# Attention and routing block on one core: values of four head pairs projected in 512-column float32r matmuls, z scaled in mid-oct, last scatters two pairs later

## The chip, the cores and the metric

The kernel runs on one core of a Trainium2 chip. The number that counts is the device time of one execution in microseconds (us). All engines of the core work in parallel and are ordered by hand with semaphores: PE (TensorE, matrix products), DVE (VectorE), ACT (ScalarE), POOL (GpSimd) and SP (SyncE, which issues most DMAs).

## The reference

```python
# x (4, 1024, 128), w_q, w_k, w_v (16 heads, 128, 64), w_o (1024, 128)
q, k, v = (einsum('bsd,hdk->bhsk', x, w) for w in (w_q, w_k, w_v))
weights = softmax(einsum('bhqk,bhmk->bhqm', q, k) / sqrt(64), axis=-1)
z = einsum('bhqm,bhmk->bhqk', weights, v)      # heads side by side: (b, s, 1024)
attn = x + einsum('bse,ed->bsd', z, w_o)
# router: softmax(xf @ Wr), argmax over 8 experts, rank of a token within its expert,
# 512 slots an expert, two matmuls with relu per expert, scaled by the share, added back
x = x + attn(layernorm(x));  x = x + ffn(layernorm(x))
```

All of it is in float32. Where the kernel has a product in the type float32r (F32R) it first splits both factors in a high part and the rest, and adds three products: high by rest, rest by high and high by high.

## The kernel before

The 4 batches have 16 heads each. A **pair** is two heads of a batch, so there are 32 pairs, numbered 0 to 31, eight to a batch. `in_order` runs the function `pair(j, par, b)` of every engine for j from 0 to 31; `par` is j modulo 2 and names the buffers.

A pair has four **octs**: octs 0 and 1 belong to the first 512 queries of both heads, octs 2 and 3 to the last 512, and an oct takes half of the 1024 keys. In an oct PE makes eight `scores` (128 keys by 512 queries of one head, two matmuls of 512 columns, lines 1335 and 1336), ACT takes their exponentials into `ring` (line 784), POOL adds them up over the keys (`add_up`, line 628, fourteen adds a pair), and PE multiplies them by V (`values`, line 1349). Between these stands work for later pairs. In order, an oct of PE is:

- scores 0 to 2; `project_qk`, queries and keys of pair j+2 (lines 1259 to 1261, three F32R matmuls of 512 columns); scores 3 and 4
- in octs 0 and 2 `project_v`: half of V of pair j+1 (line 1268, four plain float32 matmuls of 128 columns); in octs 1 and 3 `project_out` (line 1382) of an earlier pair
- scores 5 to 7; `visit`, four matmuls of `max_scores` (line 1283) for the row maxima of pair j+1; the sixteen matmuls of `values`; a second `visit`. In oct 0 also `softmax_sums` (line 1367).

The two visits of an oct and `project_qk`, `project_v` and `project_out` lend each other the same PSUM banks (`ps_m`: `lent_max`, `lent_out`, `lent_turn`). A visit may start when DVE's `reduce_max` (line 1023) has read what the visit before it left, and `project_qk` waits for all reductions so far (`maxed`).

DVE in an oct: two reductions for each visit (line 1023), `low_qk` (line 1014, the rest of queries or keys, after ACT's `cast_qk`, line 737), in octs 1 and 3 `add_out` (line 1043). It also takes the reciprocals of the softmax sums in four quarters a pair (`recip`, line 1028) and multiplies z by them (`scale_z(j, h)`, line 1037, h being the half of the queries). Between the two, SP spreads the reciprocals over partitions (`spread_sums`, line 473, eight DMAs). Before the change `scale_z(j - 1, 0)` stands behind the second reductions of oct 3, and `scale_z(j - 2, 1)` behind those of oct 0.

SP loads, in each pair, the weights of pair j+2 (`load_weights`, lines 395 to 397: w_q, w_k and w_v, 64 KB each), and then issues the `place` DMAs (lines 448 to 455), which carry the queries and keys from `qk_high` and `qk_rest` to the four operand buffers; six follow a cast. SP takes its work in order, and so a DMA issued before them delays them. The buffers `qk_high` are two, so the next cast (line 737) waits until the DMAs that read the last but one have ended; the last of these is line 451, keysB.

Tokens are normalised for a batch before its pairs (`early(j, ahead)` says for which). After a batch's pairs its second half, the router, follows within later pairs. `routed(j, role)` gives the batch whose step `role` falls into pair j: moments are `a`, roots `b`, turning and logits `c` (DVE then: `choose`, lines 970 to 976, and `shift`, line 1093), ranks and four scatters `d` (`find_slots`, lines 991 to 996), four more scatters `e`, all three batches two pairs apart. `ROUTE_FROM` is the pair of the first `a`.

```python
        def early(j, ahead):
            return j + ahead if 1 <= j + ahead < B else None
        ROUTE_FROM = PAIRS - 9
```

At the start, before pair 0, PE makes the first row maxima and runs idle matmuls (`spin`, line 1241) while transfers are under way.

## Time and profile before

| what | value |
| --- | --- |
| three runs | 1523.64, 1524.18, 1525.06 us (median 1524.18) |
| the profiled execution's time | 1522.48 us |
| its span (first to last instruction) | 1520.5 us |
| mean granted TensorE clock | 0.993 |
| busy: PE, POOL, DVE, ACT | 1488.0, 1209.4, 976.2, 793.2 us |

The span is the stretch that the profile shows; the execution's own time has 2.0 us more around it. Rows are given as start us, duration us, engine, line, operation, tile written <- tiles read, and in square brackets the idle time of the engine ahead of the row and what released it. PE's matmuls overlap, so a row of PE is read by its start: the next row's start less its own is what it costs.

### The profile page before, as it was taken

To read this page: it belongs to the slowest core of one execution; us is meant where nothing else is said; L and a number is where in the kernel's file an instruction comes from. 1 tells how busy PE (TensorE), PEld (TensorE's weight loads), DVE (VectorE), ACT (ScalarE), POOL (GpSimd) and SP (SyncE) were. 2 spreads that over 40 slices of the span, in tenths; PEclk is the share of its full clock that TensorE was granted. 3 is DMA by queue.
4 is the path that set the end of the run, shared out by engine and by line. 5 is a ranking of instruction groups with operands and counts; after the bars stand their busy time and mean duration, and the time that the engine had idled before them with its cause. 6 is when DMAs were issued, how large, how long until landed. Compare 5 with 4: busy or idle time off the path is not lost.

```text
span 1520.5 us, 22014 instructions
## 1 busy us (share of the span) xinstructions
PE 1488.0 (98%) x7472; PEld 863.8 (57%) x7472; DVE 976.2 (64%) x1236; ACT 793.2 (52%) x1549; POOL 1209.4 (80%) x672
## 2 busy tenths in 40 slices
PE   8999999999999999999999999999999999999896
PEld 5555555555555555555555555555555555555485
DVE  6667665666666666676666656667667676666552
ACT  4566645455555555555546454555554555545341
POOL 5889877798777777798777777888877989979544
PEclk9999999999999999999999999999999999999898
DMA  6334444443344443432344444433443443340420
GB/s 146 87 77 94 109 99 103 107 100 71 80 97 101 108 92 84 98 84 66 89 102 99 102 94 91 91 77 72 97 101 86 112 95 82 74 97 15 137 79 32
DMA packets 125518, 137.90 MB, mean 91 GB/s; under 512 B 44330, under 2 KB 69421, under 8 KB 125408
## 3 DMA queue, kind: packets, MB, share of 16 engines
q1 hardware_dynamic: 119008, 130.26, 37.2%
q0 software_dynamic: 2048, 4.10, 0.8%
q10 hardware_dynamic: 4352, 2.13, 0.5%
q8 instruction: 61, 1.00, 0.3%
q14 instruction: 49, 0.40, 0.1%
HBM read 16.81 MB, written 8.45 MB: 17 GB/s over the span
## 4 chain that ended last, share of the span: by engine, by line
PE 92%; DVE 3%; POOL 2%; issue 1%; ACT 1%; another core or an unknown queue 0%; DMA 0%; POOLq 0%; ACTq 0%; DVEq 0%
PE ps_w L1349 28%; PE ps_w L1335 17%; PE ps_w L1336 15%; PE ps_m L1283 11%; PE ps_m L1268 4%; PE ps_m L1382 4%; PE ps_w L1367 2%; PE ps_m L1259 2%; PE ps_m L1260 2%; PE ps_m L1261 2%; DVE mxw L1023 1%; POOL acc L628 1%; DVE z L1037 1%; PE ps_w L1622 1%; PE ps_w L1683 1%
## 5 line engine op out<-in xcount | busy, mean ns | idle before, releaser
L628 POOL TENSOR_TENSOR acc<-acc,ring 128x1024 f32<-128x1024 f32 x382 | 917.6, 2402 | 51.3 <-ACT ring L784 3.4
L1023 DVE TENSOR_REDUCE mxw<-ps_m 128x1 f32<-128x1024 f32 x512 | 602.9, 1219 | 356.4 <-PE ps_m L1283 352.0
L784 ACT ACTIVATE ring<-ps_w 128x512 f32<-128x512 f32 x1024 | 544.7, 597 | 246.4 <-PE ps_w L1336 244.2
L1349 PE MATMUL ps_w<-ring,V 128*64 128x512 f32 x2048 | 467.7, 598 | 0.0
L1335 PE MATMUL ps_w<-queriesA,keysA 128*128 128x512 f32 x1024 | 432.3, 422 | 2.0 <-ACT ring L784 1.1
L1336 PE MATMUL ps_w<-queriesB,keysB 65*128 65x512 f32 x1024 | 406.9, 397 | 0.0
L628 POOL TENSOR_TENSOR acc<-ring 128x1024 f32<-128x1024 f32 x64 | 152.2, 2378 | 180.1 <-PE ps_w L1367 172.3
L1349 PEld LDWEIGHTS ps_w<-ring,V 128*64 128x64 f32 x2048 | 135.8, 136 | 265.4 <-issue 228.2
L1335 PEld LDWEIGHTS ps_w<-queriesA,keysA 128*128 128x128 f32 x1024 | 194.4, 190 | 90.1 <-issue 49.4
L1336 PEld LDWEIGHTS ps_w<-queriesB,keysB 65*128 65x128 f32 x1024 | 194.9, 190 | 34.1 <-issue 0.7
L1283 PE MATMUL ps_m<-keysA,queriesA 64*128 64x512 f32 x1000 | 182.9, 443 | 0.8 <-DVE one_hot_b L976 0.6
L1283 PEld LDWEIGHTS ps_m<-keysA,queriesA 64*128 64x128 f32 x1000 | 74.5, 184 | 149.0 <-issue 147.6
L764 ACT ACTIVATE z<-ps_w 128x512 f32<-128x512 f32 x64 | 38.2, 597 | 221.6 <-PE ps_w L1349 221.6
L1014 DVE TENSOR_TENSOR qk_rest<-ps_m,qk_high 128x512 fp32r<-128x512 f32 x123 | 85.1, 692 | 92.7 <-ACT qk_high L737 83.0
L1028 DVE RECIPROCAL sums<-sums 128x128 f32<-128x128 f32 x128 | 116.4, 931 | 0.0
L775 ACT ACTIVATE sums<-ps_w 128x512 f32<-128x512 f32 x33 | 19.7, 597 | 129.7 <-PE ps_w L1367 115.4
L737 ACT ACTIVATE qk_high<-ps_m 128x512 fp32r<-128x512 f32 x123 | 73.5, 598 | 10.7 <-PE ps_m L1261 3.3
L1382 PEld LDWEIGHTS ps_m<-wo,z 128*128 128x128 f32 x496 | 65.0, 191 | 6.4 <-DVE mxw L1023 1.0
L1268 PEld LDWEIGHTS ps_m<-wst,hT 128*128 128x128 f32 x496 | 65.1, 191 | 5.7 <-DVE mxw L1023 0.2
L1382 PE MATMUL ps_m<-wo,z 128*128 128x128 f32 x496 | 65.6, 275 | 0.1
L1268 PE MATMUL ps_m<-wst,hT 128*128 128x128 f32 x496 | 65.5, 275 | 0.0
L664 POOL DMA_INDIRECT out<-ye,ring x32 | 31.1, 972 | 33.2 <-DVE ye L1192 26.4
(193 smaller groups left out, 974.6 us busy)
## 6 DMA issues: line engine op xcount, KB each, us to landing
queriesA<-qk_high SPq DMA_DIRECT2D x248, 128.0 KB
keysB<-qk_high SPq DMA_DIRECT2D x124, 128.0 KB
keysA<-qk_rest SPq DMA_DIRECT2D x124, 128.0 KB
queriesB<-qk_rest SPq DMA_DIRECT2D x124, 128.0 KB
by_sums<-sums SPq DMA_DIRECT2D x240, 64.0 KB, 2.0
keysA<-qk_high SPq DMA_DIRECT2D x93, 128.0 KB
tokens_by_slot<-blank ACTq DMA_DIRECT2D x16, 130.0 KB, 3.2
ring<-tokens_by_slot SPq DMA_DIRECT2D x8, 260.0 KB, 5.5
```

Source lines behind the costliest of these rows:

```text
L628: pool.tensor_tensor(acc[h][:, :], before, P_both(kt), ALU.add).then_inc(summed, 1)
L737: act.activation(qk_high[s][:, :], bank, ACT.Copy).then_inc(qk_cast, 1)
L784: act.activation(P_tile(kt, p), ps_s[k % 3][:, :], ACT.Exp, scale=SCALE).then_inc(exp_done, 1)
L1014: dve.tensor_tensor(qk_rest[s][:, :], qk_bank(j, use), qk_high[s][:, :].bitcast(F32), ALU.subtract).then_inc(qk_low, 1)
L1023: dve.tensor_reduce(mxw[h][:, p * HT + qt:p * HT + qt + 1], ps_m[p][:, :], AX_X, ALU.max).then_inc(maxed, 1)
L1028: dve.reciprocal(sums[:, c], sums[:, c]).then_inc(recip_done, 1)
L1268: mm = pe.matmul(bank[:, i * P:(i + 1) * P], hT[:, t:t + P], wst[par][:, 4 * DK:6 * DK], start=True, stop=True)
L1283: mm = pe.matmul(ps_m[p][:, kh * HALF:(kh + 1) * HALF], queriesA[par][p][r, at:at + P], keysA[par][p][r, kh * HALF:(kh + 1) * HALF], start ...
L1335: pe.matmul(ps_s[k % 3][:, :], keysA[par][p][:, t], queriesA[par][p][:, c], start=True, stop=False)
L1336: pe.matmul(ps_s[k % 3][:, :], keysB[par][p][:, t], queriesB[par][p][:, c], start=False, stop=True).then_inc(scores_ready, 1)
L1349: mm = pe.matmul(ps_z[p * DK:(p + 1) * DK, :], V[par][:, kt * P + p * DK:kt * P + (p + 1) * DK], P_tile(kt, p), start=(kt == 0), stop=(kt ...
L1382: mm = pe.matmul(bank[:, i * P:(i + 1) * P], z[j % 2][h][:, i * P:(i + 1) * P], wo[j % 3][:, :], start=True, stop=True)
```

## The change

- From pair 4 on V is not made pair by pair. For each group of four pairs `project_tile(g, t, bank)` makes V of a tile of 128 tokens for all four pairs at once: three F32R matmuls with 512 columns, for eight tiles a group. Six tiles stand in the last pair of the group before (two in octs 0 and 2, one in octs 1 and 3), two in oct 0 of the group's first pair. A tile in `lent_max` stands between scores 3 and 4, one in `lent_out` or `lent_turn` behind scores 4. The other octs have nothing in that place but `project_out`. Pairs 0 to 3 are as before.
- w_v of a group is loaded by `load_group` (64 and 192 KB) in the pairs 1, 5, ..., 25, between `load_weights` and the `place` DMAs; `load_weights` itself has one DMA less and waits for `w_low_split`. ACT splits a group's w_v in oct 1 of the pairs 2, 6, ..., 26 (`split_high_values`), POOL at h=1, kt=2 of the same pairs (`split_low_values`). `V` is one buffer with five places.
- `scale_z(j - 2, 0)` stands in mid oct 0 and `scale_z(j - 2, 1)` in mid oct 2, behind `low_qk` and ahead of the second reductions. `recip` of the last quarter moves from oct 1 to mid oct 2.
- `h_rows` is one buffer and hT holds two batches; the normalisation of batches 1, 2 and 3 falls into pairs 4b-4 to 4b-2, with four pairs between batches.
- `ROUTE_FROM` is 22 and no longer 23: `a` to `d` come one pair earlier, `e` stays where it was, two pairs behind `d`.
- Ahead of pair 0 the spins are 5 and 1 and no longer 9 and 3.

```diff
-        h_rows = [sb(f"h_rows{i}", [P, QT, D]) for i in range(2)]
+        h_rows = sb("h_rows", [P, QT, D])
...
-        hT = sb("hT", [P, T])
+        hT = sb("hT", [P, 2 * S])
...
-        V = [sb(f"V{i}", [P, KT * P]) for i in range(2)]
+        V = sb("V", [P, 5 * KT * P])
+        wv = sb("wv", [P, 4 * P])
+        wv_high, wv_low = (sb(n, [P, 4 * P], F32R) for n in ("wv_high", "wv_low"))
...
         def early(j, ahead):
-            return j + ahead if 1 <= j + ahead < B else None
...
-        ROUTE_FROM = PAIRS - 9
+            b, odd = divmod(j + ahead + 3, GROUP)
+            return b if odd == 0 and 1 <= b < B else None
+        GROUP = 4
+        GROUPS = PAIRS // GROUP
+        IN_LAST = {0: [(0, lent_max), (1, lent_out)], 1: [(2, lent_turn)], 2: [(3, lent_max), (4, lent_out)],
+                   3: [(5, lent_turn)]}
+        IN_FIRST = {0: [(6, lent_max), (7, lent_out)]}
+        def single_values(j):
+            return j < GROUP
+        def value_tiles(j, oct):
+            g, i = divmod(j, GROUP)
+            if i == GROUP - 1 and g + 1 < GROUPS:
+                return [(g + 1, t, bank) for t, bank in IN_LAST[oct]]
+            return [(g, t, bank) for t, bank in IN_FIRST.get(oct, [])] if i == 0 and g > 0 else []
+        def values_no(g, t):
+            return KT * g + t + 1
+        def place_of(j):
+            g, i = divmod(j, GROUP)
+            return 0 if g % 2 == 1 and i == GROUP - 1 else 1 + i
+        def V_of(j, kt, p):
+            at = (place_of(j) * KT + kt) * P + p * DK
+            return V[:, at:at + DK]
+        def loads_of(j):
+            k = j // 2
+            return 48 * min(k + 1, GROUP // 2) + 32 * max(k + 1 - GROUP // 2, 0)
+        ROUTE_FROM = PAIRS - 10
         def routed(j, role):
-            b, odd = divmod(j - ROUTE_FROM - "abcde".index(role), 2)
+            b, odd = divmod(j - ROUTE_FROM - "abcd-e".index(role), 2)
             return b if odd == 0 and 0 <= b < B - 1 else None
...
                     view = wst[par][:, 0:4 * DK].rearrange("p (t h k) -> p h t k", h=2, t=2)
                 sp.dma_start(view[:, :, 0, :], wq_d[:, 2 * hp:2 * hp + 2, :]).then_inc(w_loaded[par], 16)
                 sp.dma_start(view[:, :, 1, :], wk_d[:, 2 * hp:2 * hp + 2, :]).then_inc(w_loaded[par], 16)
-                sp.dma_start(wst[par][:, 4 * DK:6 * DK].rearrange("p (h k) -> p h k", h=2),
-                             wv_d[:, 2 * hp:2 * hp + 2, :]).then_inc(w_loaded[par], 16)
+                if single_values(j):
+                    sp.dma_start(wst[par][:, 4 * DK:6 * DK].rearrange("p (h k) -> p h k", h=2),
+                                 wv_d[:, 2 * hp:2 * hp + 2, :]).then_inc(w_loaded[par], 16)
+            def load_group(g):
+                h = 2 * GROUP * (g % 2)
+                order = [(h, 2), (h + 2, 6)] if g % 2 == 0 else [(h + 6, 2), (h, 6)]
+                if g > 1:
+                    sp.wait_ge(wv_low_split, g - 1)
+                for c, (h, n) in zip((slice(0, P), slice(P, 4 * P)), order):
+                    sp.dma_start(wv[:, c].rearrange("p (h k) -> p h k", h=n),
+                                 wv_d[:, h:h + n, :]).then_inc(wv_loaded, 16)
...
-                    sp.wait_ge(v_done, 2 * j + 2)
+                    if single_values(j):
+                        sp.wait_ge(v_done, 2 * j + 2)
+                    else:
+                        sp.wait_ge(w_low_split, j - 1)
                     load_weights(j + 2, par)
+                if j % GROUP == 1 and (j + 3) // GROUP < GROUPS:
+                    load_group((j + 3) // GROUP)
...
             def split_low_tokens(b, g):
                 pool.wait_ge(high_split, 2 * b + g + 1)
-                c, at = slice(g * HALF, (g + 1) * HALF), b * S + g * HALF
-                pool.tensor_tensor(h_low[:, c], hT[:, at:at + HALF], h_high[:, c].bitcast(F32),
+                c = slice(g * HALF, (g + 1) * HALF)
+                pool.tensor_tensor(h_low[:, c], hT_of(b, g), h_high[:, c].bitcast(F32),
...
+            def split_low_values(g):
+                pool.wait_ge(wv_high_split, g)
+                pool.tensor_tensor(wv_low[:, :], wv[:, :], wv_high[:, :].bitcast(F32),
+                                   ALU.subtract).then_inc(wv_low_split, 1)
...
                         if routed(j, "d") is not None and h == 1 and kt % 2 == 1:
                             scatter(routed(j, "d"), [kt // 2])
+                        if j % GROUP == 2 and (j + 2) // GROUP < GROUPS and (h, kt) == (1, 2):
+                            split_low_values((j + 2) // GROUP)
                         if routed(j, "e") is not None and (h, kt) == (0, 1):
...
+                    act.wait_ge(low_split, 2 * (b - 1))
+                    act.wait_ge(v_done, 2 * GROUP)
+                act.activation(hT_of(b, g), turn_bank(b, g), ACT.Copy).then_inc(hT_ready, 1)
...
+                act.wait_ge(residual_ready, b)
+                act.wait_ge(h_turned, 2 * b)
...
@@ -745,13 +815,28 @@
                 act.wait_ge(hT_ready, 2 * b + g + 1)
                 if b > 0:
                     act.wait_ge(qk_done, 4 * HP * b - 2 + 2 * g)
-                c, at = slice(g * HALF, (g + 1) * HALF), b * S + g * HALF
-                act.activation(h_high[:, c], hT[:, at:at + HALF], ACT.Copy).then_inc(high_split, 1)
+                    act.wait_ge(v_done, values_no(2 * b - 1, KT - 1))
+                c = slice(g * HALF, (g + 1) * HALF)
+                act.activation(h_high[:, c], hT_of(b, g), ACT.Copy).then_inc(high_split, 1)
...
             def copy_v(j, par, half, bank):
                 act.wait_ge(v_done, 2 * j + half + 1)
-                act.activation(V[par][:, half * HALF:(half + 1) * HALF], bank,
-                               ACT.Copy).then_inc(v_copied, 1)
+                at = place_of(j) * KT * P + half * HALF
+                act.activation(V[:, at:at + HALF], bank, ACT.Copy).then_inc(v_copied, 1)
...
+            def split_high_values(g):
+                act.wait_ge(wv_loaded, 32 * g)
+                if g > 1:
+                    act.wait_ge(v_done, values_no(g - 1, KT - 1))
+                act.activation(wv_high[:, :], wv[:, :], ACT.Copy).then_inc(wv_high_split, 1)
+            def copy_v_tile(g, t, bank):
+                act.wait_ge(pv_done, OCTS * (GROUP * g - 1))
+                act.wait_ge(v_done, values_no(g, t))
+                at = 1 - g % 2
+                act.activation(V[:, :].rearrange("p (s k c) -> p s k c", s=5, k=KT)[:, at:at + GROUP, t, :],
+                               bank.rearrange("p (s c) -> p s c", s=GROUP), ACT.Copy).then_inc(v_copied, 1)
...
-                    if oct in (0, 2) and not last:
+                    if oct in (0, 2) and single_values(j + 1):
                         copy_v(j + 1, nxt, oct // 2, lent_out)
+                    for made in value_tiles(j, oct):
+                        copy_v_tile(*made)
...
+                    if j % GROUP == 2 and (j + 2) // GROUP < GROUPS and oct == 1:
+                        split_high_values((j + 2) // GROUP)
...
+                    if oct in (0, 2) and j >= 2 and not last:
+                        scale_z(j - 2, oct // 2)
+                    if oct == 2 and not first and not last:
+                        recip(j - 1, 1, 3)
...
-                    if oct == 0 and j >= 2:
+                    if oct == 0 and last:
                         scale_z(j - 2, 1)
-                    if oct == (0 if last else 3) and not first:
+                        scale_z(j - 1, 0)
+                    if oct == 3 and known(j, LAST - 1):
                         scale_z(j - 1, 0)
                     if oct == 1 and not first:
                         recip(j - 1, 1, 2)
+                    if oct == 1 and last:
                         recip(j - 1, 1, 3)
...
+            def project_tile(g, t, bank):
+                b, c = GROUP * g // HP, slice(t * P, (t + 1) * P)
+                pe.wait_ge(wv_low_split, g)
+                pe.wait_ge(low_split, 2 * b + t // HT + 1)
+                pe.matmul(bank, h_low[:, c], wv_high[:, :], start=True, stop=False)
+                pe.matmul(bank, h_high[:, c], wv_low[:, :], start=False, stop=False)
+                pe.matmul(bank, h_high[:, c], wv_high[:, :], start=False, stop=True).then_inc(v_done, 1)
...
-                if oct == 0:
+                if single_values(j) and oct == 0:
                     pe.wait_ge(v_copied, 2 * j + 2)
+                elif not single_values(j) and oct < 2:
+                    pe.wait_ge(v_copied, values_no(j // GROUP, (HT if oct == 0 else KT) - 1))
...
                         mm = pe.matmul(ps_z[p * DK:(p + 1) * DK, :],
-                                       V[par][:, kt * P + p * DK:kt * P + (p + 1) * DK], P_tile(kt, p),
+                                       V_of(j, kt, p), P_tile(kt, p),
...
-                    if not last and oct in (0, 2):
+                    if oct in (0, 2) and single_values(j + 1):
                         project_v(j + 1, nxt, oct // 2, next_b, lent_out)
+                    for made in tiles:
+                        if made[2] is not lent_max:
+                            project_tile(*made)
...
-                        if not last and oct in (0, 2):
+                        if oct in (0, 2) and single_values(j + 1):
                             pe.wait_ge(v_copied, 2 * (j + 1) + oct // 2 + 1)
+                        for g, t, _ in tiles:
+                            pe.wait_ge(v_copied, values_no(g, t))
...
-            spin(9, ps_s[0])
+            spin(5, ps_s[0])
             first_visit(5, 1)
-            spin(3, ps_s[0])
+            spin(1, ps_s[0])```

PE in oct 0 of pair 3, behind the last matmul of `project_qk`; L1335 and L1336 (L1439 and L1440) are scores, L1268 is `project_v`, L1372 to L1374 are `project_tile`. Before:

```order
L1261 MATMUL ps_m<-h_high,w_high 128x512
L1335 MATMUL ps_w<-queriesA,keysA 128x512
L1336 MATMUL ps_w<-queriesB,keysB 128x512
L1335 MATMUL ps_w<-queriesA,keysA 128x512
L1336 MATMUL ps_w<-queriesB,keysB 128x512
L1268 MATMUL ps_m<-wst,hT 128x128 x4
L1335 MATMUL ps_w<-queriesA,keysA 128x512
```

Now:

```order
L1357 MATMUL ps_m<-h_high,w_high 128x512
L1439 MATMUL ps_w<-queriesA,keysA 128x512
L1440 MATMUL ps_w<-queriesB,keysB 128x512
L1372 MATMUL ps_m<-wv_high,h_low 128x512
L1373 MATMUL ps_m<-wv_low,h_high 128x512
L1374 MATMUL ps_m<-wv_high,h_high 128x512
L1439 MATMUL ps_w<-queriesA,keysA 128x512
L1440 MATMUL ps_w<-queriesB,keysB 128x512
L1372 MATMUL ps_m<-wv_high,h_low 128x512
L1373 MATMUL ps_m<-wv_low,h_high 128x512
L1374 MATMUL ps_m<-wv_high,h_high 128x512
L1439 MATMUL ps_w<-queriesA,keysA 128x512
```

The four short matmuls behind scores 4 are gone, and two tiles of three long ones stand ahead of and behind scores 4.

DVE from the end of oct 1 to the second reductions of oct 2 in an early pair; L1028 (L1117) is `recip`, L1023 (L1112) `reduce_max`, L1014 (L1103) `low_qk`, L1126 `scale_z`. Before:

```order
L1028 RECIPROCAL sums<-sums 128x128 [waits sums_copied] x2
L1023 TENSOR_REDUCE mxw<-ps_m 128x1 [waits m_done1]
L1023 TENSOR_REDUCE mxw<-ps_m 128x1 [waits m_done0]
L1014 TENSOR_TENSOR qk_rest<-ps_m,qk_high 128x512 [waits qk_cast,low_placed0]
L1023 TENSOR_REDUCE mxw<-ps_m 128x1 [waits m_done1]
```

Now:

```order
L1117 RECIPROCAL sums<-sums 128x128 [waits sums_copied]
L1112 TENSOR_REDUCE mxw<-ps_m 128x1 [waits m_done1]
L1112 TENSOR_REDUCE mxw<-ps_m 128x1 [waits m_done0]
L1103 TENSOR_TENSOR qk_rest<-ps_m,qk_high 128x512 [waits qk_cast,low_placed0]
L1126 TENSOR_TENSOR z<-by_sums,z 128x512 [waits z_copied,spread1]
L1117 RECIPROCAL sums<-sums 128x128 [waits sums_copied]
L1112 TENSOR_REDUCE mxw<-ps_m 128x1 [waits m_done1]
```

One reciprocal has gone from the end of oct 1 to mid oct 2, and a `scale_z` stands there ahead of it.

SP in pair 5, from `place_max` (L461, L518) to the first `place` DMAs (L448 and L449, L505 and L506). Before:

```order
L461 DMA queriesB<-mxt 1x4x128
L395 DMA wst<-in_L_attn_w_q 128x2x64 [waits v_done]
L396 DMA wst<-in_L_attn_w_k 128x2x64
L397 DMA wst<-in_L_attn_w_v 128x2x64
L448 DMA keysA<-qk_high 64x512 [waits qk_cast,scores_ready]
```

Now:

```order
L518 DMA queriesB<-mxt 1x4x128
L440 DMA wst<-in_L_attn_w_q 128x2x64 [waits w_low_split]
L441 DMA wst<-in_L_attn_w_k 128x2x64
L453 DMA wv<-in_L_attn_w_v 128x2x64 [waits wv_low_split]
L453 DMA wv<-in_L_attn_w_v 128x6x64
L505 DMA keysA<-qk_high 64x512 [waits qk_cast,scores_ready]
```

The pair's own w_v load has gone, and two loads of a group's w_v stand ahead of the `place` DMAs.

## Rows read from the trace of the kernel before

**Rows 1.** The page, busy time of the engines over the span

```profile
PE 1488.0 (98%) x7472; PEld 863.8 (57%) x7472; DVE 976.2 (64%) x1236; ACT 793.2 (52%) x1549; POOL 1209.4 (80%) x672
```

**Rows 2.** Busy by window: steady pair 13, and an oct without projections

```profile
603.22:646.23 43.01, 43.01 (x216) 24.42 (x216) 27.60 (x28) 23.59 (x47) 34.17 (x16) 1.00 0.39 87
62.98:72.69 9.71, 9.71 (x46) 4.96 (x44) 5.50 (x7) 4.70 (x10) 9.07 (x5) 1.00 0.17 39
```

**Rows 3.** Timeline of PE, oct 2 of pair 13

```profile
615.72 0.39 PE L1259 MATMUL ps_m<-h_high,w_low 128*128 128x512 f32 x1
...
616.42 0.40 PE L1335 MATMUL ps_w<-queriesA,keysA 128*128 128x512 f32 x1
...
617.35 1.05 PE L1268 MATMUL ps_m<-wst,hT 128*128 128x128 f32 x8
...
618.48 0.40 PE L1336 MATMUL ps_w<-queriesB,keysB 65*128 65x512 f32 x1
...
619.74 0.73 PE L1283 MATMUL ps_m<-keysA,queriesA 64*128 64x512 f32 x4
...
623.98 0.73 PE L1283 MATMUL ps_m<-keysA,queriesA 64*128 64x512 f32 x4
```

**Rows 4.** Timeline of DVE in the same pair

```profile
612.39 1.75 DVE L1028 RECIPROCAL sums<-sums 128x128 f32<-128x128 f32 x2
...
617.40 0.69 DVE L1014 TENSOR_TENSOR qk_rest<-ps_m,qk_high 128x512 fp32r<-128x512 f32 x1 [0.74 <-ACT qk_high L737]
...
643.78 0.68 DVE L1037 TENSOR_TENSOR z<-by_sums,z 128x512 f32<-128x512 f32 x1
```

**Rows 5.** Timeline of POOL in the same pair

```profile
611.31 9.93 POOL L628 TENSOR_TENSOR acc<-acc,ring 128x1024 f32<-128x1024 f32 x4
...
646.23 2.39 POOL L628 TENSOR_TENSOR acc<-ring 128x1024 f32<-128x1024 f32 x1 [7.26 <-PE ps_w L1367]
```

**Rows 6.** Timeline of DVE and POOL in pair 14, where tokens are split

```profile
675.17 1.26 POOL L616 TENSOR_TENSOR h_low<-hT,h_high 128x512 fp32r<-128x512 f32 x1
676.39 2.93 DVE L1037 TENSOR_TENSOR z<-by_sums,z 128x512 f32<-128x512 f32 x1
676.40 7.68 POOL L628 TENSOR_TENSOR acc<-acc,ring 128x1024 f32<-128x1024 f32 x3
```

**Rows 7.** Timeline, SP's queue and ACT, start of pair 14

```profile
631.87 0.60 SPq L397 DMA_DIRECT2D wst<-in_L_attn_w_v  x1
...
634.44 0.60 SPq L451 DMA_DIRECT2D keysB<-qk_high  x1
...
637.70 0.60 ACT L737 ACTIVATE qk_high<-ps_m 128x512 fp32r<-128x512 f32 x1
```

**Rows 8.** The same at the start of pair 27

```profile
1198.71 0.60 SPq L451 DMA_DIRECT2D keysB<-qk_high  x1
...
1201.57 0.60 ACT L737 ACTIVATE qk_high<-ps_m 128x512 fp32r<-128x512 f32 x1 [0.68 <-DMA keysB<-qk_high]
```

**Rows 9.** Timeline of DVE and PE at `choose` of the first batch

```profile
1137.87 0.22 DVE L970 TENSOR_REDUCE routing_columns<-ps_m 128x8 f32<-128x64 f32 x1 [2.04 <-PE ps_m L1403]
...
1139.53 0.73 PE L1283 MATMUL ps_m<-keysA,queriesA 64*128 64x512 f32 x4 [0.20 <-DVE one_hot_b L976]
```

**Rows 10.** Timeline of DVE and PE at `find_slots` of the first batch

```profile
1160.42 0.17 DVE L996 SCALAR_TENSOR_TENSOR scatter_at<-ps_m,routing_columns 128x8 int32<-128x8 f32 x1
...
1161.00 0.73 PE L1283 MATMUL ps_m<-keysA,queriesA 64*128 64x512 f32 x4
```

**Rows 11.** Timeline of POOL in pair 28, and the last four scatters of a batch

```profile
1256.45 2.39 POOL L628 TENSOR_TENSOR acc<-ring 128x1024 f32<-128x1024 f32 x1 [4.32 <-PE ps_w L1367]
...
1296.81 0.99 POOL L603 DMA_INDIRECT tokens_by_slot<-x,scatter_at  x1 [0.17 <-issue]
...
1301.63 2.41 POOL L628 TENSOR_TENSOR acc<-ring 128x1024 f32<-128x1024 f32 x1
```

**Rows 12.** Timeline at the start, PE's spins and SP's queue

```profile
25.79 2.17 PE L1241 MATMUL ps_w<-ident 128*128 128x128 f32 x18
26.28 1.36 SPq L461 DMA_DIRECT2D queriesB<-mxt  x2
27.68 0.53 SPq L448 DMA_DIRECT2D keysA<-qk_high  x1
```

**Rows 13.** Waits of PE: waiter, releaser, total us, times, longest

```profile
PE ps_m L1259 <- DVE mxw L1023: 1.6, 4, 0.6
```

26 lines of the change are left out of this document (17 added, 9 removed).

## The prediction

> **What bounds the kernel now.** I read the page's busy times first, then a window of one steady pair, then the timelines of the engines in it, then the waits. PE is busy for 1488.0 of 1520.5 us [rows 1]. In the steady pair it is busy for all of its 43.01 us, at full clock, while DVE is busy for 27.60, ACT for 23.59 and POOL for 34.17 [rows 2]. So what PE issues sets the pace, and time taken from PE's stream is time gained for as long as no other engine is late. The timelines show how near the others are. POOL stands idle for 7.26 us before each pair's first add [rows 5]. ACT makes the cast of line 737 in its turn [rows 7], and only in one of the shown places does it wait 0.68 for a transfer [rows 8]. DVE has its slack around the visits, and PE waits for it in few places [rows 9, 13].
>
> The sum below is made against the profiled execution, 1522.5 us. The median of the runs shown, 1524.2, is 1.7 above it, and I add that at the end.
>
> **1. Project_v against project_tile (PE, the gain).** In the steady pair project_v starts at 617.35 and the score behind it, whose first matmul overlaps it, has its second one at 618.48. Three plain score steps of 0.23 in their row (615.72 to 616.42 is three matmuls, 0.70 us) put the price of project_v at 1.13 less 0.23, about 0.89 [rows 3]. As a check: an oct without it takes 9.71 [rows 2] and the mean oct of the pair, which holds half a project_v, half a project_out and a project_qk, 10.75. A tile of three F32R matmuls of 512 columns has the very shape of project_qk, 0.70 [rows 3]. 56 halves go (28 pairs with two) and 56 tiles come (7 groups of 8), so the gain is 56 x (0.885 - 0.70) = **-10.4**. Bounds: -8.4 (0.85 for the one) to -11.2 (0.90).
>
> That row also bears on a rule of the Trainium skill ("TensorE: Matmul & The Clock Gate", Back-to-back issue gap), which gives about 81 ns for a sustained matmul of 128 columns and 131 ns for one of 512. By it the same swap would gain 56 x (8 x 0.081 - 3 x 0.131) = 14.3 us, an estimate. The trace has 234 ns for 512 columns of this float32r kind and does not agree, so the rule enters nothing.
>
> **2. Spins at the start.** 18 records take 2.17 us [rows 12], two to a spin, so 6 fewer spins are 12 records, 1.45 us. But the first scores also need the transfers of place_max, issued from 26.28 and followed by the place DMAs [rows 12]. The bounds are -1.45 and 0; I take the middle, **-0.7**.
>
> **3. Waits for z.** PE waits 1.6 us in four places ahead of project_qk for the last reduction [rows 13], some of them behind a slow scale_z at an oct's end. With z scaled in mid-oct these can go: **-1.0**, between 0 and -1.6.
>
> **4. The group's loads.** In the pairs 1, 5, ..., 25 SP issues two DMAs where it issued one, 0.64 us an issue (four of them lie between 631.87 and 634.44) [rows 7]. Everything behind them on SP is late by that: the six place DMAs. The last of them that a cast waits for is keysB. In the steady case it is issued at 634.44 and the cast runs at 637.70, 3.26 later [rows 7]. In the late case issue to cast is 2.86, with a wait of 0.68 [rows 8]. So the slack is 0.4, and 0.64 - 0.4 = 0.25 us of lateness is left. A late cast holds back ACT's next exponentials, and PE's score 6 waits for them, one to one. Seven loads: 7 x 0.25 = **+1.8**. Below: 0, if ACT's own backlog hides it. Above: the 192 KB are ahead of keysB in the queues; if they add a full us, 1.3 for each, 9 in all.
>
> **5. Scale_z in mid oct 2.** This is the change's dangerous place. Scale_z takes 0.68 when POOL is idle, but 2.93 at 676.39, where an add of POOL began at 676.40 [rows 4, 6]. It is done about 0.6 after the add that was running has ended, so it waits for POOL's running instruction. In oct 2 POOL always adds. The steady pair: low_qk ends at 617.40 + 0.69 = 618.09; POOL's four adds from 611.31 take 2.48 each [rows 5], so a boundary is at 611.31 + 3 x 2.48 = 618.76, 0.67 later. Scale_z would be done at 618.76 + 0.68 = 619.44, and the reciprocal (1.75 / 2 = 0.88) [rows 4] at 620.32. With project_v gone, both visits come 0.89 earlier, the next at 623.98 - 0.89 = 623.09 [rows 3]. Two reductions of 2.36 in all, from 620.32, end at 622.7. That leaves 0.4 us: **0** in the steady pair. The work that hides it is PE's sixteen values matmuls. If scale_z comes over 0.67 later, it misses that boundary, loses 2.48 more, and the visit waits 2.48 - 0.4 = 2.1.
>
> A rule of the Trainium skill ("GPSIMD Engine Reference", § 8 Key points) says that GpSimd shares its SBUF interfaces with VectorE, and that this tells on VectorE instructions with two SBUF inputs. The trace agrees: scale_z is one, 2.93 against 0.68 us. It speaks against this change, and the prices here and in the rivals are taken from the rows alone.
>
> Where the phase is not the steady one:
> - Pairs 6, 14 and 22 split tokens: line 616 takes 1.26 of POOL in mid-oct [rows 6] and moves the boundary by as much. I put the end of the reductions 0.7 behind the visit, 3 x 0.7 = **+2.1** (0 to 2.4 in all, then other boundaries are met).
> - Pairs 24, 26 and 28 have `choose` and `shift` in oct 2. Before, DVE was idle for 2.04 ahead of choose, and PE's visit still waited for 0.20 [rows 9]. The logits now come 0.89 earlier, but scale_z with its wait and the reciprocal, 0.67 + 0.68 + 0.88 = 2.2, come first. 2.2 + 0.2 - 2.04 + a part of 0.89 makes between 0.4 and 1.2: 0.7 x 3 = **+2.1**; a missed boundary in all three would make it 8.
> - Pairs 25, 27 and 29 have find_slots in oct 0, with slack 161.00 - 160.59 = 0.4 (both + 1000) [rows 10]. Where there is no tile (25 and 29) the visit comes 0.89 earlier and scale_z adds 0.68 less what DVE idled: 0.7 x 2 = **+1.4**; 0 to 2.3.
>
> **6. POOL.** POOL keeps its work, so with the pair shorter by at most 1.8 its idle time falls from 7.26 to about 5.5, and by a few tenths more for the adds that scale_z touches. Both groups of four scatters now fall into the pairs 27 and 29: 45.2 us from 1256.45 to 1301.63 for adds and eight scatters, against 43.0 - 1.8 = 41.2 for pair 29. The excess of 4.0 meets the 4.32 of idle before it [rows 11]: **+0.3**, at most 4.
>
> **7. What costs nothing.** The tiles' copies on ACT (0.60) replace those of V. The splits of w_v on ACT and POOL (once a group, about 1 us) lie in POOL's idle time and ACT's 19 us a pair. A tile in lent_max ahead of scores 4 waits for reductions that end 0.2 before it by the steady timeline; it is bounded by 0 and 0.3 a tile, for 14 tiles 4 us, and I take 0. Hidden by ACT's three queued exponentials.
>
> **Sum.** -10.4 - 0.7 - 1.0 + 1.8 + 2.1 + 2.1 + 1.4 + 0.3 = -4.4. 1522.5 - 4.4 = 1518.1 for a profiled execution, 1518.1 + 1.7 = **1519.8** for the median.
>
> **Rivals.**
> - *All stalls are hidden.* DVE and ACT queue up differently once PE is faster, and a stall in one oct gives the next more slack. Then 4, 5 and 6 fall to 0 or 1: -12.1, so 1512 to 1516. For it: 15.4 us of idle DVE a pair [rows 2]. Against it: the 0.4 us at the visit.
> - *Scale_z misses POOL's boundary* (slower). One mechanism at one place, mid oct 2: 2.1 us for each pair in which low_qk ends over 0.67 late against POOL's adds. 12.1 / 2.1: from six such pairs on the gain is gone. With the other terms it takes four beyond the ones counted to pass 1528, and with six 1519.8 + 12.6 = 1532. For it: rows 6, where just this happened, and the tiles of the pairs 4g+3, which change the phase. Against it: POOL's phase is set by PE's softmax_sums, so both shift together.
> - *The transfer is the price, not the issue.* 1.3 in each of the seven load pairs, 9.1 where I have 1.8: 1519.8 + 7.3 = 1527, no change. For it: casts do wait for keysB already [rows 8]. A page of the Trainium skill ("DMA: Bandwidth & Descriptors", Specifications) says that descriptors under 512 bytes do not reach line rate; these loads have runs of 256 bytes. No row here separates that.
> - *POOL becomes the bound in the last pairs*, 4 us, 1524.
>
> **How the numbers follow.** A median of this kernel tells a difference from none at about 0.2%, 3.05 us: faster is below 1521.1, slower above 1527.2. The forecast (1517 to 1522) has 0.47, of which 0.12 lies within 0.2%. Stalls hidden: 0.25, faster. Scale_z behind POOL: 0.13, of which 0.11 slower. The transfer: 0.10, 0.07 no change and 0.03 slower. POOL and others: 0.05, no change 0.04, slower 0.01. So faster is 0.35 + 0.25 = 0.60, same 0.12 + 0.02 + 0.07 + 0.04 = 0.25, slower 0.15. The range from 1513 to 1527 leaves out a tail of the hidden case (0.04), half of the transfer case (0.05) and scale_z behind POOL (0.11), 0.2 together.
>
> **What would show it.** Right: steps of PE at a tile of 0.70, a steady pair of 41.2 us without tiles; scale_z in oct 2 of about 1.3 us, done 0.6 behind an add's end; waits of PE ahead of visits in the pairs 6, 14, 22 and in the routing pairs, each under 1; a wait of ACT for keysB in the pairs 1, 5, ... of a few tenths. Wrong: tiles of another price; PE waits of 2 us for reductions in steady pairs; casts late by 1 or more; POOL without idle time in pair 30. The prediction fails most easily at the 0.4 us of slack at the visit and at the load's price, since both are differences of rows of another phase.

## The result and the profile after

| kernel | runs | median us | of before on the same chip | ratio, 95% interval |
| --- | --- | --- | --- | --- |
| changed, first measurement | 5 | 1517.08 (1512.81 to 1521.67) | 1524.99 | 0.9959 [0.9944, 0.9974] |
| changed, measured again | 12 | 1518.59 (1512.75 to 1524.30) | 1523.43 | 0.9971 [0.9954, 0.9987] |

The change makes the kernel faster by 0.3 to 0.4%. The forecast was 1519.8 in 1513 to 1527; the change gained 7.9 and 4.8 us where the sum had 4.4.

The changed kernel's runs lie 9 to 12 us apart, and the granted clock orders them. The first five, time and mean clock: 1512.81 at 0.995, 1516.61 at 0.992, 1517.08 at 0.993, 1520.77 and 1521.67 at 0.988. Over 12 runs a straight line has 1.3 us for each 0.001. So I compare kernels in a second way too, by the mean over the runs of time multiplied by clock, which takes out most of what the clock adds: 1504.4 and 1504.3 for the changed kernel in its two measurements, and 1511.4 to 1512.8 for before in three (19 to 35 runs each, standard deviation of a run 1.2 to 1.6). By that measure the change is worth 7.1, on the same chip. It takes out a lower clock whatever brought it about, a kernel's own waits too, so I give both measures. One of twelve runs of the kernel e6 below took 3848.12 us, at a clock of 1.00; its row has the other eleven.

The profiled execution is the slowest of the five, 1521.67 us. Its busy times (the line that answers to [rows 1]):

```profile
span 1519.5 us, 21578 instructions
...
PE 1484.4 (98%) x7180; PEld 842.8 (55%) x7180; DVE 998.1 (66%) x1236; ACT 794.0 (52%) x1556; POOL 1220.3 (80%) x679
```

Windows of it, the first four each from one project_qk of oct 2 to that of the next pair: with three tiles (from pair 18), with five (19), without any (20), and that of pair 28. The last begins in pair 30, which has no project_qk of oct 2. Columns are as in [rows 2].

```profile
828.66:872.12 43.46, 43.46 (x208) 24.12 (x208) 28.74 (x29) 23.48 (x47) 35.99 (x18) 1.00 0.43 99
872.12:916.83 44.71, 44.71 (x214) 25.45 (x214) 27.54 (x29) 24.62 (x49) 33.73 (x15) 1.00 0.38 85
916.83:958.35 41.52, 41.52 (x200) 22.30 (x199) 28.56 (x29) 21.87 (x44) 34.18 (x16) 1.00 0.43 98
...
1267.35:1314.94 47.59, 45.33 (x225) 25.80 (x225) 32.67 (x45) 22.85 (x45) 40.70 (x22) 0.96 0.36 85
...
1357.94:1400.00 42.06, 39.03 (x159) 21.12 (x158) 26.87 (x26) 16.16 (x31) 34.00 (x18) 0.84 0.08 21
```

A pair without tiles takes 41.52 where one of before took 43.01 [rows 2]: two halves of project_v cost 1.49, or **0.75** each. Five tiles cost 44.71 - 41.52 = 3.19 and three 43.46 - 41.52 = 1.94, together 5.13 for a group of eight, **0.64** each. PE is busy for all of it: no stall in a steady pair.

Why both are less than the rows said is seen in PE's timeline, oct 2 of pair 19 with two tiles, then oct 2 of pair 20 with none:

```profile
872.82 0.40 PE L1439 MATMUL ps_w<-queriesA,keysA 128*128 128x512 f32 x1
...
873.28 0.40 PE L1372 MATMUL ps_m<-wv_high,h_low 128*128 128x512 f32 x1
...
873.99 0.40 PE L1439 MATMUL ps_w<-queriesA,keysA 128*128 128x512 f32 x1
...
875.15 0.39 PE L1439 MATMUL ps_w<-queriesA,keysA 128*128 128x512 f32 x1
875.38 0.40 PE L1440 MATMUL ps_w<-queriesB,keysB 65*128 65x512 f32 x1
...
918.95 0.50 PE L1439 MATMUL ps_w<-queriesA,keysA 128*128 128x512 f32 x1
919.29 0.40 PE L1440 MATMUL ps_w<-queriesB,keysB 65*128 65x512 f32 x1
```

The tile itself takes 0.71 (873.28 to 873.99), as forecast. But in the oct that has nothing behind scores 4, the first matmul of scores 5 takes 0.34 to the next (918.95 to 919.29), and behind a tile 0.23 (875.15 to 875.38): about 0.1 us that whatever stands in this place hides. Behind a project_v it was hidden too, in the eight matmuls before it [rows 3]. Each oct that lost its project_v paid it again; with two tiles in an oct it is hidden once for two.

Scale_z in mid oct 2 of a steady pair, DVE and POOL:

```profile
914.89 7.72 POOL L695 TENSOR_TENSOR acc<-acc,ring 128x1024 f32<-128x1024 f32 x3
...
918.51 0.69 DVE L1103 TENSOR_TENSOR qk_rest<-ps_m,qk_high 128x512 fp32r<-128x512 f32 x1 [0.74 <-ACT qk_high L807]
919.11 1.27 DVE L1126 TENSOR_TENSOR z<-by_sums,z 128x512 f32<-128x512 f32 x1
920.31 0.94 DVE L1117 RECIPROCAL sums<-sums 128x128 f32<-128x128 f32 x1
921.17 2.28 DVE L1112 TENSOR_REDUCE mxw<-ps_m 128x1 f32<-128x1024 f32 x2
```

It takes 1.27: it waits 0.6 for the add that is running, and the reductions end at 923.45, before the visit at 924.34. This is the place as the prediction drew it.

What the prediction did not have stands in three places near the end. First, DVE, POOL and PE in pair 29:

```profile
1299.13 2.38 POOL L695 TENSOR_TENSOR acc<-ring 128x1024 f32<-128x1024 f32 x1 [3.96 <-PE ps_w L1473]
1299.19 2.35 DVE L1095 TENSOR_TENSOR x<-routing_columns,roots 128x8 f32<-128x8 f32 x1
...
1301.45 2.34 DVE L1112 TENSOR_REDUCE mxw<-ps_m 128x1 f32<-128x1024 f32 x2
...
1302.72 0.78 PE L1355 MATMUL ps_m<-h_high,w_low 128*128 128x512 f32 x1 [1.52 <-DVE mxw L1112]
1303.30 0.63 PE L1356 MATMUL ps_m<-h_low,w_high 128*128 128x512 f32 x1
...
1303.72 0.63 PE L1357 MATMUL ps_m<-h_high,w_high 128*128 128x512 f32 x1
```

A product of 8 columns (line 1095, in `find_shares`) takes 2.35 us, and 0.17 or 0.18 the other four times; it came 0.06 behind the start of an add and ended 0.03 behind its end. The reductions are late, PE waits for 1.52, and then its matmuls stand 0.42 apart (1303.30 to 1303.72) and not 0.23: the granted clock fell to its lower level, 1.2 of 2.4 GHz. This wait is a matter of phase: of the profiles with z in these places it stands in this one and in e1's, and not in those of the second measurement, e2 and e12. Second, pair 30, where the last reciprocal now comes in oct 2:

```profile
1359.47 0.94 DVE L1117 RECIPROCAL sums<-sums 128x128 f32<-128x128 f32 x1
...
1360.43 5.00 SPq L530 DMA_DIRECT2D by_sums<-sums  x8
...
1366.98 0.60 ACT L860 ACTIVATE sums<-ps_w 128x512 f32<-128x512 f32 x1 [7.08 <-DMA by_sums<-sums]
...
1367.63 0.79 PE L1439 MATMUL ps_w<-queriesA,keysA 128*128 128x512 f32 x1 [1.52 <-ACT sums L860]
```

ACT may only write the next sums when SP's eight DMAs have read the last, and in pairs 30 and 31 the sums come half by half, so there is no pair of time between. PE waits 1.52, and the window that holds this place runs at 0.84. Third, the end of pair 30, where `scale_z` of pair 29 has kept its place behind the second reductions of oct 3:

```profile
1377.87 2.11 DVE L1126 TENSOR_TENSOR z<-by_sums,z 128x512 f32<-128x512 f32 x1
...
1383.91 1.38 PE L1488 MATMUL ps_m<-wo,z 128*128 128x128 f32 x8 [1.51 <-DVE mxw L1112]
```

It waits for an add of POOL, two reciprocals and the first reductions of pair 31 follow, and `project_out`, which waits for these, stands for 1.51. Before had no such wait. It is 2.10 in the second measurement's profile, 0.47 in e2's and 1.01 in that of the fastest kernel below, e11.

### The profile page after: what moved, and what is told of

It reads as the page before. It is cut to its first block, busy times and chain, and to the rows that moved or that the text cites. A ratio compares the mean times of both kernels' runs of the same rounds, so it can differ in the third digit from the quotient of the medians.

```text
span 1519.5 us, 21578 instructions
## 1 busy us (share of the span) xinstructions
PE 1484.4 (98%) x7180; PEld 842.8 (55%) x7180; DVE 998.1 (66%) x1236; ACT 794.0 (52%) x1556; POOL 1220.3 (80%) x679
## 4 chain that ended last, share of the span: by engine, by line
PE 89%; DVE 4%; POOL 2%; issue 1%; ACT 1%; SPq 1%; DMA 1%; another core or an unknown queue 0%; POOLq 0%; ACTq 0%; DVEq 0%
PE ps_w L1455 28%; PE ps_w L1439 16%; PE ps_w L1440 14%; PE ps_m L1387 10%; PE ps_m L1488 4%; POOL acc L695 2%; PE ps_w L1473 2%; PE ps_m L1355 2%; PE ps_m L1356 2%; PE ps_m L1357 2%; DVE mxw L1112 1%; PE ps_m L1372 1%; PE ps_m L1373 1%; PE ps_m L1374 1%; DVE z L1126 1%
## 5 line engine op out<-in xcount | busy, mean ns | idle before, releaser
L695 POOL TENSOR_TENSOR acc<-acc,ring 128x1024 f32<-128x1024 f32 x382 | 918.9, 2406 | 55.2 <-ACT ring L869 7.8
L1112 DVE TENSOR_REDUCE mxw<-ps_m 128x1 f32<-128x1024 f32 x512 | 601.6, 1217 | 333.6 <-PE ps_m L1387 324.4
L1439 PE MATMUL ps_w<-queriesA,keysA 128*128 128x512 f32 x1024 | 434.2, 424 | 4.2 <-ACT sums L860 1.5
L1440 PE MATMUL ps_w<-queriesB,keysB 65*128 65x512 f32 x1024 | 408.7, 399 | 0.0
L695 POOL TENSOR_TENSOR acc<-ring 128x1024 f32<-128x1024 f32 x64 | 152.0, 2376 | 163.5 <-PE ps_w L1473 155.4
L1439 PEld LDWEIGHTS ps_w<-queriesA,keysA 128*128 128x128 f32 x1024 | 195.2, 191 | 105.4 <-issue 49.5
L1440 PEld LDWEIGHTS ps_w<-queriesB,keysB 65*128 65x128 f32 x1024 | 195.9, 191 | 34.1 <-issue 0.7
L1103 DVE TENSOR_TENSOR qk_rest<-ps_m,qk_high 128x512 fp32r<-128x512 f32 x123 | 85.1, 692 | 94.2 <-ACT qk_high L807 82.5
L1117 DVE RECIPROCAL sums<-sums 128x128 f32<-128x128 f32 x128 | 120.2, 941 | 0.3 <-ACT sums L860 0.3
L860 ACT ACTIVATE sums<-ps_w 128x512 f32<-128x512 f32 x33 | 19.7, 596 | 127.3 <-PE ps_w L1473 108.1
L1126 DVE TENSOR_TENSOR z<-by_sums,z 128x512 f32<-128x512 f32 x60 | 79.2, 1320 | 0.0
L807 ACT ACTIVATE qk_high<-ps_m 128x512 fp32r<-128x512 f32 x123 | 73.5, 598 | 9.4 <-DMA keysB<-qk_high 2.1
L1488 PEld LDWEIGHTS ps_m<-wo,z 128*128 128x128 f32 x496 | 66.3, 195 | 7.7 <-DVE mxw L1112 2.2
L1488 PE MATMUL ps_m<-wo,z 128*128 128x128 f32 x496 | 66.8, 278 | 1.5 <-DVE mxw L1112 1.5
L1132 DVE TENSOR_TENSOR x<-ps_m,x 128x512 f32<-128x512 f32 x62 | 42.7, 689 | 28.1 <-PE ps_m L1488 28.0
```

The source lines that it names most:

```text
L695: pool.tensor_tensor(acc[h][:, :], before, P_both(kt), ALU.add).then_inc(summed, 1)
L807: act.activation(qk_high[s][:, :], bank, ACT.Copy).then_inc(qk_cast, 1)
L1103: dve.tensor_tensor(qk_rest[s][:, :], qk_bank(j, use), qk_high[s][:, :].bitcast(F32), ALU.subtract).then_inc(qk_low, 1)
L1112: dve.tensor_reduce(mxw[h][:, p * HT + qt:p * HT + qt + 1], ps_m[p][:, :], AX_X, ALU.max).then_inc(maxed, 1)
L1117: dve.reciprocal(sums[:, c], sums[:, c]).then_inc(recip_done, 1)
L1126: dve.tensor_tensor(z[j % 2][h][:, :], by[:, :], z[j % 2][h][:, :], ALU.mult).then_inc(z_ready, 1)
```

## The experiments

"Time x clock" is the mean over the runs, and behind it the difference to before in the same session; its standard error is 0.4 to 0.6. The kernels ran in three sessions, each on a chip of its own: e1, e3, e5 and e6 in the first, the changed kernel again, e7, e9 and e10 in the second, e2, e11, e12 and e13 in the third. Between sessions only the differences to before compare well.

| kernel | runs | median us | ratio to before, 95% | time x clock |
| --- | --- | --- | --- | --- |
| before + z in mid-oct (e6) | 11 | 1527.14 | 1.0023 [1.0006, 1.0040] | 1511.1, -1.3 |
| before + routing schedule (e7) | 12 | 1525.76 | 1.0013 [1.0001, 1.0024] | 1512.5, +1.0 |
| tiles, old z, old spins (e5) | 12 | 1526.84 | 1.0025 [1.0011, 1.0038] | 1511.6, -0.8 |
| changed, old z (e3) | 12 | 1527.59 | 1.0028 [1.0011, 1.0046] | 1510.5, -1.9 |
| changed (again) | 12 | 1518.59 | 0.9971 [0.9954, 0.9987] | 1504.3, -7.1 |
| changed, old spins (e2) | 8 | 1520.02 | 0.9972 [0.9958, 0.9986] | 1505.4, -7.3 |
| changed, reciprocal of pair 30 early (e1) | 12 | 1519.98 | 0.9976 [0.9963, 0.9990] | 1506.7, -5.7 |
| changed, loads behind the place DMAs (e12) | 12 | 1518.76 | 0.9973 [0.9956, 0.9990] | 1506.1, -6.6 |
| changed, z scaled with one operand (e9) | 6 | 1513.86 | 0.9947 [0.9932, 0.9961] | 1501.3, -10.1 |
| changed, both z in mid oct 0 (e10) | 6 | 1515.29 | 0.9953 [0.9940, 0.9966] | 1503.8, -7.7 |
| e10 + last pair's z early (e11) | 6 | **1512.27** | **0.9921 [0.9906, 0.9936]** | 1501.8, -10.9 |
| e11 + loads behind (e13) | 6 | 1513.42 | 0.9932 [0.9918, 0.9946] | 1502.1, -10.7 |

**Old places for z in the changed kernel (e3), and the tiles alone (e5).** The edit of e3; e5 also has the spins of before.

```diff
-                    if oct in (0, 2) and j >= 2 and not last:
-                        scale_z(j - 2, oct // 2)
-                    if oct == 2 and not first and not last:
-                        recip(j - 1, 1, 3)
...
-                    if oct == 0 and last:
+                    if oct == 0 and j >= 2:
                         scale_z(j - 2, 1)
-                        scale_z(j - 1, 0)
-                    if oct == 3 and known(j, LAST - 1):
+                    if oct == (0 if last else 3) and not first:
                         scale_z(j - 1, 0)
                     if oct == 1 and not first:
                         recip(j - 1, 1, 2)
-                    if oct == 1 and last:
                         recip(j - 1, 1, 3)
```

> The changed kernel with scale_z and the last reciprocal quarter back at the places of before (behind the second reductions of oct 3 and oct 0, end of oct 1). Theory that the gain is the tiles': scaling in mid-oct buys nothing in most pairs (PE is busy in 41.5 of 41.5 us there) and costs 3 to 5 us in pair 30, so this kernel is 2 to 5 us faster than the changed one, 1512 to 1515. Rival, that moving z is what pays (it removes PE's waits for reductions ahead of project_qk, 1.6 us before): 2 to 6 us slower, 1519 to 1523, with waits of PE for DVE ahead of project_qk of over 3 us in all.

> The tiles with the new routing schedule (which their PSUM banks need) alone: z scaled at the old places and the old numbers of spins. From the traces a half of project_v costs 0.755 us and a tile 0.65, so 56 of each give -5.9; waits at the start as before. Theory: 1517 to 1520 less what the place in pair 30 costs, so 1512 to 1518. Rival, that the tiles alone move nothing because the granted clock or other waits take it: 1523 to 1526.

My theory fell and the rival held, though the loss is more than it said. With z at its old places the changed kernel is 8 us slower by the medians' differences to before (+3.5 against -4.8), 5 by time x clock (-1.9 against -7.1), and the tiles with z at its old places are no faster than before by the medians. PE's waits ahead of project_qk, of e3:

```profile
PE ps_m L1349 <- DVE mxw L1112: 7.7, 8, 3.7
```

7.7 us in eight places (e5: 5.8 in eight) where before had 1.6 in four [rows 13]. The longest, as DVE, POOL and PE show it in e3:

```profile
1302.09 2.38 POOL L695 TENSOR_TENSOR acc<-ring 128x1024 f32<-128x1024 f32 x1 [3.21 <-PE ps_w L1467]
1302.22 2.79 DVE L1126 TENSOR_TENSOR z<-by_sums,z 128x512 f32<-128x512 f32 x1
...
1305.41 1.83 DVE L1095 TENSOR_TENSOR x<-routing_columns,roots 128x8 f32<-128x8 f32 x1
...
1308.42 0.80 PE L1349 MATMUL ps_m<-h_high,w_low 128*128 128x512 f32 x1 [3.73 <-DVE mxw L1112]
```

Behind the second reductions of an oct, scale_z stands right ahead of the reductions that project_qk waits for. In the kernel before, POOL was idle or about to end there, and 9 of 62 scale_z took over 1 us. With the shorter pairs 33 of 62 do. In mid-oct 40 do, but there the visit has the slack. E3's profile also has 2.77 of waiting in pair 31 (see e1), and its median clock is 0.989.

**The other parts on the kernel before (e6, e7).** e6 is the edit above the other way round, in the kernel before. e7 is this:

```diff
-        ROUTE_FROM = PAIRS - 9
+        ROUTE_FROM = PAIRS - 10
...
-            b, odd = divmod(j - ROUTE_FROM - "abcde".index(role), 2)
+            b, odd = divmod(j - ROUTE_FROM - "abcd-e".index(role), 2)
```

> The kernel before with only scale_z and the last reciprocal quarter moved into mid-oct, as in the changed kernel. Theory: scale_z waits for POOL's running add (mean 0.9 us before, 1.3 after), the pairs keep their 43.0 us, and pair 30 gets the wait of ACT for the spread sums: 1525 to 1530, so 0 to 5 us slower than before. Rival: the mid-oct place removes waits of PE and gives 1 to 3 us, 1522 to 1524.

> The kernel before with only the new routing schedule (steps a to d one pair earlier, the last four scatters where they were). With the tiles and this schedule but z at its old places the chip gave 1527, so either the schedule loses what the tiles gain, or the tiles with the earlier normalisation do. Theory: in the profile of that kernel the pairs 27 to 31 take 48.7, 46.3 and 45.2 us with scale_z of 2.8 to 3.2 behind POOL, and here the same: 1526 to 1530, 3 to 5 us slower than before. Rival: no difference (1523 to 1525), and the loss is the normalisation's in the pairs 1 to 3 and the waits ahead of project_qk.

By themselves both lose: 3.0 us and 2.3 us by the medians. For e6 that is as the theory had it; by time x clock it is 1.3 less than before, as the rival had it, and what it loses is clock (0.990 against 0.993). In its profile the stretch up to oct 2 of pair 29 is 0.9 shorter; the loss stands behind it, with waits of PE of 0.64 and 2.69 in pairs 30 and 31 and the lower clock there.

For e7 the loss is a little under the 3 to 5 that I expected. Its profile says where it lies: the visit of pair 29 waits 2.36 for find_slots, project_qk 0.77 and 1.32 in pairs 27 and 28, and pair 31 has 2.80 of waiting for the copy of the sums.

So none of the three parts alone is a gain in time: tiles with the schedule they need +2.7, z +3.0, schedule +2.3, all of them together -4.8 to -7.9. By time x clock they are -0.8, -1.3 and +1.0, together -7.1. The normalisation that moved with the tiles was not tried by itself.

**The changed kernel once more.**

> The changed kernel once more, beside the kernel before on the same chip, since its five runs lie 9 us apart. Theory: the runs differ by the granted clock alone, about 1.2 us for each 0.001 of its mean, and time multiplied by clock is 8 us less than before (1504 against 1512); so the median follows the clock it happens to get, 1516 to 1520. Rival: the change's runs differ for another reason and time multiplied by clock spreads as widely as the time.

It came out so, but for the size: 1518.59 at a median clock of 0.9905, and time x clock is the same to 0.1 and 7.1 under before, not 8. The standard deviation of a run is 4.0 us in time and 1.5 in time x clock.

**Which operand makes DVE wait (e9).** Scale_z leaves out the division by the softmax sums here.

```diff
-                dve.tensor_tensor(z[j % 2][h][:, :], by[:, :], z[j % 2][h][:, :], ALU.mult).then_inc(z_ready, 1)
+                dve.tensor_scalar(z[j % 2][h][:, :], z[j % 2][h][:, :], 0.001, None, ALU.mult).then_inc(z_ready, 1)
```

> The changed kernel, but scale_z multiplies z by a constant (one operand from SBUF in place of two) at the same places; it leaves out the division by the softmax sums. Theory: what makes scale_z wait for POOL's running add is its second SBUF operand; then all 62 take the same 0.3 to 0.7 us (mean 1.3 now), and the time falls by the waits behind it, 3 to 6 us below the changed kernel. Rival: any float32 operation of DVE between SBUF buffers waits for POOL; then the mean stays above 1 us and the time as it is.

The mechanism of the theory fell; the rival is nearer. The group of line 1126 in e9, and one case of it with POOL's adds:

```profile
L1126 DVE TENSOR_SCALAR z<-z 128x512 f32<-128x512 f32 x62 | 61.9, 999 | 0.0
...
655.07 7.46 POOL L695 TENSOR_TENSOR acc<-acc,ring 128x1024 f32<-128x1024 f32 x3
658.20 2.11 DVE L1126 TENSOR_SCALAR z<-z 128x512 f32<-128x512 f32 x1
```

With one operand it takes 0.42 at least (0.68 with two), but it still waits for POOL's add: 2.11 here, 1.0 on average. In all 29 cases of over 1 us it ends 0.28 or 0.29 behind the end of the add that was running; with two operands, in the changed kernel, 0.55 or 0.56 in all 40. The reciprocals, also from SBUF to SBUF with one operand, never do (128 of them, 0.89 to 0.95 us). Why a multiply waits and a reciprocal doesn't is open. What e9 gains, 3.0 by time x clock, goes with DVE being done earlier: PE's waits ahead of visits (line 1387) are 0.4 us in its profile, 2.6 and 2.1 in the changed kernel's two.

**The reciprocal of pair 30 (e1).**

```diff
-                    if oct == 2 and not first and not last:
+                    if oct == 2 and not first and not known(j, LAST - 1, LAST):
                         recip(j - 1, 1, 3)
...
-                    if oct == 1 and last:
+                    if oct == 1 and known(j, LAST - 1, LAST):
                         recip(j - 1, 1, 3)
```

> The changed kernel with one edit: in pair 30 the last reciprocal quarter stands at the end of oct 1 again, not in mid oct 2. Theory: in the profile after, SP can issue spread_sums of pair 29 only at 1360.43, ACT's copy of the next sums waits 7.08 us for those DMAs, PE then waits 1.5 us and runs at the lower clock for some 5 us, so this one place costs 3 to 5 us; expected 3 to 5 us faster than the changed kernel's 1517 (1512 to 1514), and no wait of ACT for by_sums over 3 us. Rival: the wait is hidden by the wait of PE for POOL's last adds, which follows at about 1409 in the kernel before; then no change (1517).

The wait for by_sums is gone (ACT waits 4.43 for PE there), but nothing is gained: -4.2 against before, and -5.7 by time x clock where the changed kernel has -7.1. The time stands one pair later, in oct 0 of pair 31:

```profile
1382.25 3.21 DVE L1126 TENSOR_TENSOR z<-by_sums,z 128x512 f32<-128x512 f32 x1
1382.51 2.39 POOL L695 TENSOR_TENSOR acc<-ring 128x1024 f32<-128x1024 f32 x1
1385.04 15.74 POOL L695 TENSOR_TENSOR acc<-acc,ring 128x1024 f32<-128x1024 f32 x6
1385.38 2.84 DVE L1126 TENSOR_TENSOR z<-sums,z 128x512 f32<-128x512 f32 x1
...
1388.32 0.60 ACT L860 ACTIVATE sums<-ps_w 128x512 f32<-128x512 f32 x1 [8.33 <-DVE z L1126]
...
1388.97 0.50 PE L1439 MATMUL ps_w<-queriesA,keysA 128*128 128x512 f32 x1 [2.78 <-ACT sums L860]
```

With PE earlier, both scale_z of the last pair now fall on POOL's adds, which in the changed kernel they missed (1.31 and 0.68). The stall that was removed had held them apart. The other profiles bear it out: e3, e5, e7 and e10, which have no such wait in pair 30, have 2.8 us of waiting for these sums in pair 31, and the changed kernel's two, e2, e9 and e12, which wait 1.3 to 1.6 us in pair 30, have 0.3 at most.

**Both z in mid oct 0 (e10), and early in the last pair (e11).** In steady pairs POOL is idle in mid oct 0. The last pair's oct 0 has POOL issuing scatters ahead of the second reductions.

```diff
-                    if oct in (0, 2) and j >= 2 and not last:
-                        scale_z(j - 2, oct // 2)
+                    if oct == 0 and j >= 2 and not last:
+                        scale_z(j - 2, 0)
+                        scale_z(j - 2, 1)
+                    if oct == 0 and last:
+                        scale_z(j - 2, 1)
+                        scale_z(j - 1, 0)
```

(e10 has the first part alone; e11 leaves out the last pair's two behind the reductions.)

> The changed kernel with both scale_z of a pair in mid oct 0, where POOL stands idle in the steady pairs, in place of one in oct 0 and one in oct 2. Theory: most scale_z then take 0.68 and the visits of oct 2 get their slack back, so 2 to 4 us faster than the changed kernel, with the stalls of the last two pairs left. Rival: the second scale_z makes DVE late at the visit of oct 0 (0.7 more there), in the pairs with find_slots above all: 0 to 3 us slower than the changed kernel.

> The kernel with both scale_z in mid oct 0, and in the last pair its two scale_z ahead of the second reductions as well, while POOL issues scatters. In the profile of the kernel with both in oct 0 these two took 3.2 and 2.8 us behind POOL's adds, the copy of the sums waited for them and PE 2.8 us for it. Theory: both take 0.68 there and PE's wait goes: 2 to 3 us less, 1512 to 1513.5. Rival: the time comes back as a longer wait for POOL's last adds, with no change from 1515.3.

e10 is 3.3 us faster than the changed kernel beside it, within the theory's 2 to 4, but only 0.5 by time x clock, which is no more than its standard error: 21 of 62 scale_z are over 1 us, and most of what it wins is clock (0.9925 against 0.9905). In e11 the last pair reads

```profile
1377.99 0.99 POOL L665 DMA_INDIRECT tokens_by_slot<-x,scatter_at  x1
...
1378.81 0.68 DVE L1126 TENSOR_TENSOR z<-by_sums,z 128x512 f32<-128x512 f32 x1
...
1379.41 0.69 DVE L1126 TENSOR_TENSOR z<-sums,z 128x512 f32<-128x512 f32 x1
...
1384.72 0.60 ACT L860 ACTIVATE sums<-ps_w 128x512 f32<-128x512 f32 x1 [4.43 <-PE ps_w L1479]
```

Both take 0.68 while POOL issues scatters, PE's 2.8 us of waiting are gone, and e11 is 1512.27, the fastest kernel here: 11 us below before, 3 below e10 by the medians and 2 to 3 by time x clock, as expected.

**The loads (e12, e13) and the spins (e2).**

```diff
-                if j % GROUP == 1 and (j + 3) // GROUP < GROUPS:
-                    load_group((j + 3) // GROUP)
                 if not last:
...
                         place(j + 1, nxt, use)
+                if j % GROUP == 1 and (j + 3) // GROUP < GROUPS:
+                    load_group((j + 3) // GROUP)
```

> The changed kernel with the loads of a group's w_v issued behind the place DMAs of the pair, not ahead of them. The prediction priced their place at 1.8 us in all (0 to 9). Theory: casts no longer wait for keysB in the pairs 1, 5, ... (1.9 us in all in a profile of the changed kernel), and the time falls by 0.5 to 1.8. Rival (the transfer, not the issue): 5 us or more less. Nothing if ACT's queue hides it.

> Both edits at once on the kernel with both scale_z in mid oct 0: the last pair's two scale_z ahead of the reductions and the group's loads behind the place DMAs. Theory: the gains add, 1511 to 1513. Rival: the edits meet in the same slack and this is no better than the better one of them.

> The changed kernel with the spins ahead of pair 0 back at 9 and 3. The prediction gave the six spins 0.7 us (0 to 1.45). Theory: 0.7 us slower than the changed kernel's 1516.8 at a clock of 0.992. Rival: the spins keep the granted clock up at the start (it fell to 0.72 between 20 and 25 us in one profile of the changed kernel, and not in that of before); then the clock is 0.001 higher and the time 0 to 1 us shorter.

The casts' waits for keysB go from 2.1 us in four places and 1.9 in three (the changed kernel's two profiles) to 0.3, but what stands behind the loads now is place_max, and PE waits for that. Of e12's waits of PE:

```profile
PE ps_w L1439 <- DMA queriesB<-mxt: 2.3, 3, 1.1
```

So nothing is gained (1518.76 against 1518.59; 1513.42 for e13 against 1512.27, where the rival of e13 held), and the transfer as such is no large price. The old spins are 1.4 us slower by the medians of two sessions and 0.2 faster by the difference to before in time x clock; 0.7 can't be told from nothing. The granted clock between 20 and 25 us was 0.50 to 0.78 in three of the five profiles with the old spins (e2, e5, e6) and in three of the nine with the new ones (after, e12, e13), 1.00 in all others: the old spins don't hold it.

## Why the prediction was right, and where it was off

- **Tiles.** -10.4 was the largest term, and it is the mis-sized one: by the windows after, seven groups of eight halves and eight tiles are 7 x (4 x 1.49 - 5.13) = -5.8. The row price of a tile was right (0.71). The price of project_v took 0.23 off for the score behind it, which takes 0.34 where nothing hides it; that 0.1 is paid in each oct that loses its project_v and gets no tile. The prediction's own check had the answer: 10.75 - 9.71 = 1.04 us, less a quarter of softmax_sums (644.98 to 645.98 in before, 1.0 a pair), is 0.79 for half a project_v and half a project_out of the same eight matmuls, so 0.79 and not 0.89. (The oct of 9.71 in [rows 2] does hold a project_qk, at 65.18.)
- **Waits for z, -1.0.** As a term it holds: 1.6 us in before, none in the profiles of e2 and of the second measurement. What it had wrong is to size them by the kernel before and add them to the tiles as a part of its own. In the kernel with the tiles they would be 7.7 us (e3), and it is the new place that keeps them from arising: 5 us by time x clock. It is not a gain against before, but without it the tiles bring nothing.
- **Scale_z in mid oct 2.** Right for steady pairs: 1.27 us, no stall, so the slower rival did not come about. The pairs 6, 14 and 22 cost 0.2, 0.2 and 0.4 over their neighbours (43.70, 43.70 and 43.89 against 43.46), 0.9 where I had 2.1. With `choose`, in pairs 24, 26 and 28, the visit waits 0.36 each time where before had 0.20: 0.5 more in all, where I had 2.1.
- **Find_slots, +1.4.** The visits of pairs 25 and 29 wait 0.46 and 0.38: 0.8. The 1.52 of pair 29 is another operation at another place: not scale_z at the visit, but find_shares' product ahead of project_qk, and it is in some profiles only.
- **The loads, +1.8.** In the profile after, five of the seven load pairs can be set beside others and take 41.6, 41.6, 42.3, 41.5, 41.5 where 41.5 is the pair without: about 1.0. The rival that the transfer is the price fell.
- **What was missed.** Pair 30's wait for the spread sums, 1.5 us (a reciprocal that moved has SP's DMAs and a buffer behind it), and the wait ahead of project_out behind pair 30's scale_z, 0.5 to 2.1. On the other side stands a wait of PE for POOL's last adds, 2.62 us at 1409.04 in the profile of before, which the profiles after do not have. A part of it is the schedule: in e7, which has the schedule alone, POOL issues four scatters fewer in pair 30 and this wait is gone. But e6, without the schedule, lacks it too, because PE has waited 3.3 us shortly before. In e11 PE has waited just 1.0 in pairs 30 and 31, and POOL is still done 1.7 us ahead of it, so there it is a gain.
- **Does the sum close?** The profile of e2 has nearly the clock of before (0.992 against 0.993); its span is 1515.1, 5.4 less. The start, up to the first F32R project_qk, is 1.4 longer. From there to project_qk of oct 2 in pair 29 lie 1256.9 us, before 1258.0, so 1.1 less: 53 of the 56 halves of project_v stood there, 3.6 of the tiles' 5.8; the new schedule brings the logits and ranks of the third batch into this stretch, 1.9 us of PE; 0.6 more are waits. The rest of the program is 5.7 less: 2.2 for the other three halves, the same 1.9, and 2.6 for POOL's wait, against 1.8 more of waiting in pairs 30 and 31 than before has there. That leaves 0.8 that I did not take apart.
- **The clock.** The sum was made at an unchanged clock. The changed kernel's median clock is 0.9905 in the twelve runs, against 0.992 of before beside them, which costs some 2 us. All three waits of 1.5 us in the changed kernel's profile have the lower level behind them, but that is not the rule here: between 60 and 1410 us the fourteen profiles have 34 waits of PE of over 1 us. The nine longest, 2.36 to 3.73, all have the lower level within 5 us behind them; of the other 25, 1.0 to 2.1, six have.

So the total was near in part by luck. The tiles were counted 4.6 us too high as a gain. The costs of the loads, the splits, choose and find_slots were counted 7.4 and came to 1.0 + 0.9 + 0.5 + 0.8 = 3.2. A gain of 2.6 that was not seen met waits of 2 to 3.6 us in pairs 30 and 31 that were not seen either. What was right as a mechanism is that PE's stream sets the pace, that the steady mid-oct place hides scale_z's wait, and that the transfer of w_v is no large price.

## What to carry to other kernels

When PE's stream gets shorter, everything that sits at a phase against another engine moves; a term read off the old phase is worth only as much as the slack beside it. Parts that each lose by themselves can gain together, so undo one part of the whole as well as trying it alone. Place a DVE operation that waits for GpSimd where GpSimd is idle or issues DMAs (e11). Look at the last pairs apart, since buffers turn over faster there. And a wait that has gone is a gain only if none has come ahead of it: here the wait taken from pair 30 (e1) brought one in pair 31, and only e11 and e13 have neither.

## What was not expected of the hardware

- A DVE product of 128 x 8 took 2.35 us, and a one-operand float32 multiply of 128 x 512 took 2.11 (0.42 alone), when a POOL add was running; reductions from PSUM and reciprocals did not wait. A scale_z that waited ended 0.55 us behind the end of the add with two operands, 0.28 with one. The add that follows is lengthened too (2.64 against 2.38 us). Scatters that POOL issues don't hold DVE up (0.68).
- The mean granted clock differs between runs of one kernel (0.986 to 0.995 for the changed one), and 0.001 of it is worth 1.0 to 1.5 us here (a straight line over the runs, in ten of twelve kernels). Five of the drops in the fourteen profiles come with no idle time of PE ahead: in e3 the pair from 1176.22 to 1224.86 took 48.64 us at 0.93 with PE busy throughout. What lowered the clock there stays open.
